# Weighted sums of two slots in one visit of TensorE, in an attention and expert block on one Trainium2 core

## The reference

```python
h = _layernorm(x, axis=-1) * (1 + ca) + sa
q = split_heads(_binlinear(x, Wq, bq))
k = split_heads(_binlinear(x, Wk, bk))
v = split_heads(_binlinear(x, Wv, bv))
att = jnp.einsum('bhtd,bhsd->bhts', q, k) * scale
att = jax.nn.softmax(att, axis=-1)
y = jnp.einsum('bhts,bhsd->bhtd', att, v)
y = y.transpose(0, 2, 1, 3).reshape(B, T, C)
return _binlinear(y, Wp, bp)
...
x = x + ga * _L0_attn_ref(h, ...)
h = _layernorm(x, axis=-1) * (1 + cb) + sb
x = x + gb * _L0_ffn_ref(h, ...)
```

## Time and profile before

| | |
|---|---|
| median of 3 runs | 728.68 us |
| the runs | 724.27 to 731.09 us |
| profiled execution: time, span | 723.38 us, 721.6 us |
| mean granted TensorE clock | 0.948 |
| PE, DVE, ACT, POOL busy | 89%, 72%, 57%, 36% of the span |
| batches begin (first score) at | 42.96, 103.20, 158.95, 220.29, 284.15, 347.03, 409.22, 468.16 us |

### The profile page before, as it was taken

One profiled execution on the slowest core, in us unless ns is written; L12 is line 12 of the kernel. 1 busy time (PEld: TensorE's weight loads), 2 busy tenths in 40 slices (PEclk: granted clock), 3 DMA queues, 4 the chain that ended last, 5 costly groups with the idle time before them and its releaser, 6 DMA issues.

```text
span 721.6 us, 11593 instructions
## 1 busy us (share of the span) xinstructions
PE 642.8 (89%) x3693; PEld 303.2 (42%) x3693; DVE 517.3 (72%) x1104; ACT 410.7 (57%) x846; POOL 262.2 (36%) x309
## 2 busy tenths in 40 slices
PE   5788999998998999799899989989998998888845
PEld 2332333333232333233233322322365788787841
DVE  5569779895887689588778868867267855564517
ACT  3145777765775577477558757657833345354420
POOL 4230041514325152432515233043164165666540
PEclk9679999998999799899989999999999999999978
DMA  3622231222232033222312212200601222222228
GB/s 95 163 52 69 80 101 49 73 76 85 63 92 92 21 101 91 66 64 85 99 30 75 73 59 62 66 31 15 183 27 45 57 78 71 77 73 74 73 67 301
DMA packets 50064, 56.92 MB, mean 79 GB/s; under 512 B 10281, under 2 KB 39243, under 8 KB 50004
## 3 DMA queue, kind: packets, MB, share of 16 engines
q1 hardware_dynamic: 42648, 43.11, 21.3%
q0 software_dynamic: 4320, 8.47, 3.5%
q10 hardware_dynamic: 3036, 4.61, 2.0%
HBM read 38.36 MB, written 17.92 MB: 78 GB/s over the span
## 4 chain that ended last, share of the span: by engine, by line
PE 68%; DVE 14%; ACT 6%; issue 5%; DMA 4%; another core or an unknown queue 1%; SPq 1%; POOL 0%; ACTq 0%; DVEq 0%; POOLq 0%
PE st L1423 15%; PE pv L1434 15%; PE mx L1408 13%; PE st L1623 9%; DVE neg_max L989 6%; ACT pt L780 3%; PE misc L1301 2%; PE mx L1567 2%; PE misc L1328 2%; PE misc L1632 2%; PE pv L1632 2%; PE misc L1334 1%; DMA even_qk<-k_parts 1%; DVE ln L946 1%
## 5 line engine op out<-in xcount | busy, mean ns | idle before, releaser
L780 ACT ACTIVATE pt<-st 128x512 f32<-128x512 f32 x496 | 282.3, 598 | 141.9 <-PE st L1423 113.2
L989 DVE TENSOR_REDUCE neg_max<-mx 128x2 f32<-128x1024 f32 x248 | 295.8, 1216 | 78.0 <-PE mx L1408 68.5
L1434 PE MATMUL pv<-pt,vs 128*32 128x512 f32 x1024 | 141.2, 625 | 0.3 <-ACT pt L780 0.3
L1423 PE MATMUL st<-even_qk 74*128 74x512 bf16 x256 | 91.9, 399 | 12.2 <-issue 7.6
L727 POOL DMA_INDIRECT results<-qs,home_u x71 | 77.5, 1092 | 60.7 <-ACT qs L909 41.5
L1423 PE MATMUL st<-qs,ks 74*128 74x512 bf16 x240 | 84.8, 395 | 11.9 <-issue 7.2
L692 POOL DMA_INDIRECT routed<-rec,row_u x64 | 63.3, 989 | 65.2 <-DVE row_u L1069 36.8
L1408 PE MATMUL mx<-even_qk 72*128 72x512 bf16 x240 | 76.0, 399 | 7.0 <-DMA even_qk<-k_parts 3.5
L1408 PE MATMUL mx<-ks,qs 72*128 72x512 bf16 x256 | 79.1, 391 | 2.7 <-DVE neg_max L989 2.4
L398 POOL TENSOR_TENSOR qk_r<-qk_f,qk_parts 128x512 f32<-128x512 f32 x15 | 17.5, 1164 | 121.4 <-DVE qk_parts L390 121.3
L1235 DVE TENSOR_TENSOR vs<-vs,st 128x256 f32<-128x256 f32 x71 | 29.7, 418 | 44.3 <-ACT vs L904 35.0
(11 more groups left out here) (199 smaller groups left out, 841.0 us busy)
## 6 DMA issues: line engine op xcount, KB each, us to landing
ks<-routed SPq DMA_DIRECT2D x71, 65.0 KB
even_qk<-q_parts SPq DMA_DIRECT2D x48, 96.0 KB
qs<-q_parts SPq DMA_DIRECT2D x48, 96.0 KB
ks<-k_parts SPq DMA_DIRECT2D x48, 96.0 KB
even_qk<-k_parts SPq DMA_DIRECT2D x42, 96.0 KB
q_parts<-qk_parts SPq DMA_DIRECT2D x21, 128.0 KB
k_parts<-qk_parts SPq DMA_DIRECT2D x7, 384.0 KB
x_in<-L_attn_x SPq DMA_DIRECT2D x8, 256.0 KB, 3.3
```

Of the source, the lines that this page charges most:

```text
L780: act.activation(pt[n % 2][:, hh, :], score_bank(b, n, hh), ACT.Exp, scale=SCALE).then_inc(exp_done, 1)
L989: dve.tensor_reduce(neg_max[g % 2][:, hh, 2 * half:2 * half + 2], mx_bank[half][:], AX_X, ALU.max, negate=True).then_inc(mx_free, 1)
L1423: pe.matmul(score_bank(b, n, hh), ks[b.par][0:STACK, h, j * P:(j + 1) * P], qs[b.par][0:STACK, h, :], start=True, stop=True).then_inc(st_f ...
L1434: last = pe.matmul(pv_bank[32 * hh:32 * (hh + 1), :], vs[b.par][:, j, HG * g + hh, :], pt[n % 2][:, hh, :], start=(n % Y_SLOTS == 0), stop ...
```

## The change

The weighted sums of two slots are made together, at the end of every even slot: slot n takes those of slots n - 2 and n - 1, and odd slots have none. A buffer of exponentials must live longer for this, so there are three, used in turn by the number of the slot over the whole program. The copy of the strips moves one slot later on ACT, from slot 8 to slot 9 and from slot 0 to slot 1 of the next batch. At the end of the program the last two quads stand after the last slot.

```diff
@@ -17,6 +17,7 @@
+PT_RING = 3
@@ -70,7 +71,7 @@
-        pt = [sb(f"pt{i}", [P, HG, T]) for i in range(2)]
+        pt = [sb(f"pt{i}", [P, HG, T]) for i in range(PT_RING)]
@@ -777,7 +778,7 @@
                 for hh in range(HG):
                     act.wait_ge(st_full, HG * quad + hh + 1)
-                    act.activation(pt[n % 2][:, hh, :], score_bank(b, n, hh), ACT.Exp, scale=SCALE).then_inc(exp_done, 1)
+                    act.activation(pt[quad % PT_RING][:, hh, :], score_bank(b, n, hh), ACT.Exp, scale=SCALE).then_inc(exp_done, 1)
@@ -841,7 +842,7 @@
                     exponentials(b, n)
-                    if n == 0 and not first:
+                    if n == 1 and not first:
                         evacuate_y(b.plus(-1), YG - 1)
@@ -866,7 +867,7 @@
-                    if n == Y_SLOTS:
+                    if n == Y_SLOTS + 1:
                         evacuate_y(b, 0)
@@ -1431,7 +1432,7 @@
-                    last = pe.matmul(pv_bank[32 * hh:32 * (hh + 1), :], vs[b.par][:, j, HG * g + hh, :], pt[n % 2][:, hh, :],
+                    last = pe.matmul(pv_bank[32 * hh:32 * (hh + 1), :], vs[b.par][:, j, HG * g + hh, :], pt[quad % PT_RING][:, hh, :],
@@ -1547,10 +1548,12 @@
-                    if n > 0:
-                        products(b, n - 1)
-                    elif not first:
-                        products(b.plus(-1), SLOTS - 1)
+                    if n % 2 == 0:
+                        for k in (SLOTS - 2, SLOTS - 1) if n == 0 else (n - 2, n - 1):
+                            if n > 0:
+                                products(b, k)
+                            elif not first:
+                                products(b.plus(-1), k)
@@ -1579,6 +1582,7 @@
+            products(B_LAST, SLOTS - 2)
             products(B_LAST, SLOTS - 1)
```

## The result

The changed kernel takes **771.53 us** (median of 4 runs, 768.84 to 775.22), the kernel before 726.47 beside it: a ratio of 1.062, with the interval 1.057 to 1.068. The forecast was 744, with 762 as its upper end. The direction was right, the size was not.

What follows compares the result with a forecast made beforehand. Bound: PE, ACT and DVE in a ring with two score and two maxima banks. Batch terms 2 + 3.4 + 9 + 1 = 15.4, or 19, taken as +17, gave 744 us; own range 733 to 755, 8-in-10 range 722 to 762.

Steps and rivals of the forecast that it cites:

- The sum: Whole attention: batch costs add to 15.4 us, 19 on a dearer reading, taken as +17; forecast median 744.
- The saving: At the quads: each pair of slots enters and leaves them once less, a pair lasts 1.88 us, saving 0.21.
- The banks, undisturbed batch, +3.4: Batch without stall: missing odd-slot quads expose waits for ACT's and DVE's banks, 0.9 + 0.55 + 5 x 0.4 us.
- Batches 2 to 6: +1.8 each: Stalled batches: 3.4 less 0.9 (slot 3 released by the stall) and 0.7 (half clock covers banks), five batches +9 us.
- Batch 0, +2: First batch: slots 1 to 4 bound by DVE in both orders, 0; the other five pairs +0.4 us each.
- Batch 7, +1 to slot 8 and 0 behind it: Last batch: +1 us to slot 8; in its last slots four banks cover a pair of quads, so 0.
- The stall grows, some 3.5 us of low clock in each of six batches: PE idle with less work in hand, low clock lasting as long again: 17 + 20, median 765 us; chance 0.10.
- The saving comes through: Banks do not bind in odd slots, so the saving stands: -13, median 716 us; chance 0.08.
- the stall goes: Slots 2 to 4, batches 2 to 6: two quads and later strips could avoid it, -32 + 20, median 717; chance 0.06.
- a clock that is low in other places than before: Sign in the profile after that would show the forecast wrong; no size given.

Runs made afterwards that it cites:

- short exponentials and reductions: Changed kernel with scatter split, exponentials over half their columns and maxima over half the keys from the fourth slot on: 654.12 us on the second chip.
- Moving the stall: Changed kernel with POOL's scatter of a batch moved half a batch later, to slots 11 to 14: 772.50 us, ratio 1.059.
- the extra fills: Changed kernel with scatter split, the second fill of each odd slot made twice into the same bank: 729.17 us on the second chip, ratio 1.098.

## Why the prediction was wrong in its size

**The sum.** The forecast of 744 is 728.7 + 15.4, although the text takes +17, which would give 746. The measured difference is +45 in the medians and +48.5 in the spans of the profiled executions.

**The saving: right.** 0.21 a pair rested on a pair of quads of 1.88; it is 1.86 at full clock. At half clock two adjacent quads hold PE for 3.6, as the earlier trace rows suggest. The 1.2 GHz that the prediction puts beside the clock stands in no trace. They show a granted share, 1.00 or 0.50, and from a score to the next matmul 0.22 us at 1.00 and 0.43 at 0.50 (301.39 to 301.82 in the kernel before).

**The banks, undisturbed batch, +3.4: nearly right.** Batch 1 lost 4.0, in 59.73 against the forecast's "about 59". By slots of batch 1: 1 to 4, +1.3 (forecast 0.9 + 0.4); 5 and 6, +0.6 (0.55); 7 to 12, +0.4 to 0.5 a pair (0.4); 13 and 14, +0.9, where 0.4 stood; 15 and 0 together, 0 (0). Slots 13 and 14 make up the difference. Odd slots last 2.15 to 2.5 (forecast 2.1 to 2.6), even ones 4.8 to 5.6 (4.9 to 5.6). The short exponentials and reductions show that both engines' banks bind: eased together they take the loss of a batch from 4.0 to 2.0, and eased exponentials alone shorten three of the eight stretches. What I left aside is that DVE's banks bind in more pairs than those of slots 1, 2, 5 and 6: also in those that end in slots 0, 10 and 14, which only shorter reductions made shorter. The waits for reductions rose from 20.6 to 32.3.

**"Batches 2 to 6: +1.8 each": the step that failed.** They lost 5.8 each on average (5.6, 4.4, 5.4, 6.0, 7.4), 28.8 us together where the sum has 9. I took 0.9 off since slot 3 is released by the stall, and 0.7 since half clock would hide the banks. In batch 4 slots 0 to 4 lost 1.9 against 2.4 in batch 1, so that the discount was 0.5 and not 1.6: the stall ended 2.0 us after the last scatter, not with it, and the low clock behind it lasted 10.2 us and took in a pair of quads. And I had put no price at all on a clock that falls in ordinary slots. It falls once more in each of these batches, twice in batch 2, for about 3.4 us, in which a pair of quads costs up to 3.6 instead of 1.86. On the third chip the changed kernel's batches with a fall take 61.38 and the one without 59.74: **1.64 us a fall**, all of it busy time of PE (56.71 against 55.07), none of it waiting. Its nine falls, one of them twice as long, are some 16 of the 45 us by which its attention is longer there than that of the order before with its scatters split beside the loads; about 29, what is left, I put down to the banks. How the two share the loss on the first chip was not measured.

**Batch 0, +2: it lost 6.1.** Zero for slots 1 to 4 was wrong. On the third chip slots 1 to 4 cost 4.6 more than before, with two falls in them, and slots 9 and 10 cost 2.2 with another.

**Batch 7, +1 to slot 8 and 0 behind it: it lost 7.1.** A pair of quads in low clock lies in slot 8 (6.30 against 3.00). Of the last slots I wrote that four banks cover a pair; slots 13 and 14 took 1.08 + 3.64 = 4.72 where the earlier trace rows have 3.94, slots 9 and 10 took 4.98 for 4.49. The four banks are emptied while a pair of quads streams, and then ACT has nothing to do: it stood 1.19 us before the first exponential of slot 13. Scores 2 and 3 of slot 14 then wait for the exponentials 2 and 3 of slot 13, which run only behind that pair.

**The rivals.** "The stall grows, some 3.5 us of low clock in each of six batches", 765, with a chance of 0.10, had the right kind of cost and nearly the measured time, for the smaller part of the reason. The low clock behind the stalls did grow, by 13.8 us; in ordinary slots it grew by 30.8. Moving the stall changed nothing (1.059), and on the third chip the loss is 47 us with no stall. "The saving comes through" and "the stall goes" are out. The list of what would prove me wrong did name "a clock that is low in other places than before"; it should have been a term of the sum.

**What makes the clock fall.** In the order before, an ordinary slot ends with a quad, and between two quads lie some 2.0 to 3.3 us of scores, fills and an errand. In the new order 4.5 to 6.7 us do. There the granted clock falls at some of the pairs; with a quad put back in the middle of six of the eight stretches it does not fall at all from batch 1 on, and with shorter work on ACT and DVE it does not either. So the falls come of the new order, but what decides them is not shown. PE's busy share alone is not it: a stretch of 3.40 us with 2.93 busy, without quads, was followed by a clock of 0.50, one with 2.86 busy and a quad in it by 1.00, and of two alike stretches of 5.40 us, both 5.09 busy, one was followed by a fall. Long waits of PE are not it either: in the 3.40 us ahead of the pair in slot 12 of batch 3 it is idle for 0.31 in all, with 0.18 as the longest wait the profile names, and the clock falls. That many short waits do it is a guess of mine. For it: both cures took waits away. Ahead of slot 12 PE is idle for 0.31 us as changed, for 0.19 with short exponentials and reductions, and for 0.00 with the third quad, while the extra fills brought it to 0.47 and more falls. The longest stretch speaks against it, with 0.88 idle in slots 1 and 2 and no fall. Whether there is more in the quads that keeps the clock up, the four column groups at once or the fp32 operands, no run here shows.

**Open.** The stall of the first chip goes where the scatters go; when their run is cut in two, it goes away in the kernel before, and in the changed one a short stall in slot 5 is left; whether its cause is the run's length, or something beside it, and why two chips lack it, was not settled. The extra quads also shorten PE's idle time, so that their effect on the clock may be that in part or altogether. No run fills PE's waits in their place with work other than quads.

## What to carry to other kernels

Before grouping work to save transitions, ask what the scattered pieces covered: a quad of 1.0 us at the end of a slot was the time in which two engines emptied their banks, and taking it away cost about 0.7 a pair in a batch at full clock, of which the 0.21 saved left a loss of 0.5. Ask also what the clock does where the heaviest matmuls are bunched: here it fell to 0.50 in some batches just when a pair of quads began (at 293.2 in batch 3, where the pair then took 3.59 us in place of 1.92), and that showed as the same work taking longer (PE busy +26 us in all), not as a wait. Price each discount ("hidden by the stall") against a batch where the hiding thing is absent, and see whether it survives there.

## What the runs showed of the hardware that was not expected

- Extra matmuls cost no time here: six quads more in every batch left it at 712.9 us against 712.9.
- TensorE shown busy for 3.09 of 3.40 us was followed by a granted clock of 0.50. Of two like stretches, both busy for 5.09 of 5.40 us, one was followed by it and the other by 1.00.
- Eight indirect scatters in a row on GpSimd, 1.26 us apart, went on one chip with idle times of 2.3 to 4.1 us on ACT and DVE in the kernel before, waiting for matmuls whose records had ended (such as the 3.21 at 322.62 in the changed kernel), and with low clock behind. Cut into runs of four they had none of this in the kernel before, and this was worth 34 us of 727; in the changed kernel some 1 to 2 us a batch of such waiting was left, in slot 5.
- The same kernel took 725 to 727 us on one chip and 664 and 665 on two others.
